# Penalty rows of the two key stacks loaded in unit 13 of SyncE's program, ahead of the stores of the chunk's keys

## The reference, cut to what matters

```python
x = layernorm(x + attn(x))                                # 16 heads, one K and one V for all of them
Q, K, V = x @ Wq.T + bq, ctx @ Wk.T + bk, ctx @ Wv.T + bv  # 1024 queries, 6404 keys, 16 heads of 8
scores = where(mask == 0, -1e9, Q K^T / sqrt(8))
x = layernorm(x + softmax(scores) V @ Wo.T + bo)
x = layernorm(x + top1_expert(x))
```

## Time and profile before

| | |
|---|---|
| median of three runs | 472.44 us (471.43 to 472.73) |
| profiled execution: span | 468.0 us |
| profiled execution: time around its span | not on the page; its only time is the span |
| mean granted TensorE clock | 0.981 |
| PE busy | 441.4 us, 94% |
| DVE (VectorE) busy | 400.8 us, 86% |
| ACT (ScalarE) busy | 359.8 us, 77% |
| POOL (GpSimd) busy | 246.1 us, 53% |
| DMA | 56.07 MB, mean 120 GB/s |

### The profile page before, as it was taken

The page is one execution under the profiler, slowest core; times in us unless marked ns, Lnnn a source line. Parts: engine busy times, 40 slices in busy tenths (PEclk is TensorE's granted clock), DMA queues, the critical chain, the costliest instruction groups (busy, mean ns, idle before and its releaser), DMA issues.

```text
span 468.0 us, 10772 instructions
## 1 busy us (share of the span) xinstructions
PE 441.4 (94%) x3885; PEld 175.9 (38%) x3887; DVE 400.8 (86%) x506; ACT 359.8 (77%) x704; POOL 246.1 (53%) x382
## 2 busy tenths in 40 slices
PE   7999989999999999899999999999999999999973
PEld 2533333333334433233344333333344334343441
DVE  5989989999899698689998999999999899962175
ACT  6328878698867777688868888888868688878843
POOL 4836878976899404222446643454438154321364
PEclk9889999999999999999999999999999899999998
DMA  5859977679760172211322345322222122111001
GB/s 131 322 125 315 278 258 251 265 245 377 260 267 14 36 125 68 67 50 39 89 73 69 114 87 106 90 61 58 81 58 69 39 59 62 50 41 40 5 12 36
DMA packets 24596, 56.07 MB, mean 120 GB/s; under 512 B 6443, under 2 KB 15929, under 8 KB 22493
## 3 DMA queue, kind: packets, MB, share of 16 engines
q0 software_dynamic: 7536, 37.91, 24.9%
q1 hardware_dynamic: 16424, 17.24, 14.2%
q10 hardware_dynamic: 580, 0.20, 0.2%
HBM read 45.60 MB, written 9.18 MB: 117 GB/s over the span
## 4 chain that ended last, share of the span: by engine, by line
PE 69%; DVE 15%; DMA 5%; POOL 4%; issue 4%; ACT 2%; ACTq 0%; DVEq 0%; POOLq 0%
PE O L1491 26%; PE ST L1727 14%; PE RT L1720 7%; PE ST L1518 7%; DVE mxs L938 7%; PE RT L1506 4%; DVE mxc L955 3%; POOL big L612 3%; DMA big<-in_mask 2%; DMA Qs<-mxr 2%; PE RT L1613 2%; PE ST L1620 1%; PE O L1469 1%; DVE mxc L956 1%; PE RT L1583 1%
## 5 line engine op out<-in xcount | busy, mean ns | idle before, releaser
L1290 ACT ACTIVATE prob<-ST 128x512 f32<-128x512 f32 x512 | 280.9, 599 | 59.1 <-PE ST L1518 27.4
L938 DVE TENSOR_REDUCE mxs<-RT 128x2 f32<-128x1024 f32 x128 | 152.8, 1222 | 12.8 <-PE RT L1506 11.7
L955 DVE TENSOR_REDUCE mxc<-RT 128x2 f32<-128x1024 f32 x128 | 152.4, 1219 | 6.6 <-PE RT L1720 6.4
L1727 PE MATMUL ST<-Qs,Kc 64*128 64x512 f32 x320 | 117.8, 451 | 0.0
L1720 PE MATMUL RT<-Kr,Qs 64*128 64x512 f32 (+1 forms) x384 | 114.1, 405 | 2.2 <-issue 2.2
L1491 PE MATMUL O<-prob,vst 128*9 128x256 f32 x1280 | 99.9, 384 | 1.7 <-ACT prob L1279 0.5
L1518 PE MATMUL ST<-Qs,Kself 64*128 64x512 f32 x256 | 96.2, 447 | 2.5 <-DMA Qs<-mxr 2.4
L684 POOL DMA_DIRECT2D Kr<-kd x96 | 47.8, 503 | 85.9 <-PE RT L1720 70.8
L1506 PE MATMUL RT<-Kself,Qs 64*128 64x512 f32 x256 | 88.7, 462 | 2.2 <-DVE Kself L915 0.9
L1491 PE MATMUL O<-prob,Vs 128*9 128x256 f32 x1024 | 80.2, 385 | 1.2 <-ACT osb L1234 0.3
L1727 PEld LDWEIGHTS ST<-Qs,Kc 64*128 64x128 f32 x320 | 50.6, 185 | 66.3 <-issue 36.6
(11 more groups left out here) (219 smaller groups left out, 326.8 us busy)
## 6 DMA issues: line engine op xcount, KB each, us to landing
big<-in_mask POOLq DMA_DIRECT2D x16, 1664.0 KB, 7.6
Kc<-kd POOLq DMA_DIRECT2D x64, 80.0 KB, 2.3
Kr<-kd POOLq DMA_DIRECT2D x64, 64.0 KB, 2.1
od_s<-osb SPq DMA_DIRECT2D x16, 128.0 KB, 2.3
kd<-Vx SPq DMA_DIRECT2D x4, 512.0 KB, 6.7
Qs<-qd_x SPq DMA_DIRECT2D x8, 256.0 KB
od_x<-osb SPq DMA_DIRECT2D x14, 128.0 KB, 1.7
Qs<-qd_s SPq DMA_DIRECT2D x12, 128.0 KB, 5.9
```

What stands on the lines that cost most here:

```text
L938: freed(v.tensor_reduce(mxs[:, h % 2, c2, :].rearrange("p (f t) -> p f t", f=2)[:, :, q], bank[:, :].rearrange("p (f k) -> p f k", f=2), A ...
L955: return v.tensor_reduce(o[:, :, u % 4], src, AX.X, ALU.max)
L1290: freed(nc.scalar.activation(prob[:, s % SLOTS, f * HALF:(f + 1) * HALF], bank[:, :], ACT.Exp))
L1727: mm = mmul(o[:, :], Kc[STACK[f], b * P:(b + 1) * P], Qs[STACK[f], j, :], start=True, stop=not gen, skip_group_check=True)
```

## The change

In SyncE's loop the two waits and the two loads move from the turn `h == 14`, behind `more_keys()`, into the turn `h == 13`, right behind the five stores to `pd`. `more_keys()` stays in `h == 14`.

```diff
                 if h == 13:
                     sp.wait_ge(S("pen_made"), 1)
                     for k, c in enumerate((*range(CHUNKS - 4, CHUNKS), CHUNKS - 5)):
                         load(pd[:, k * KC:(k + 1) * KC], penr[...], "pen_out")
-                if h == 14:
-                    more_keys()
                     sp.wait_ge(S("pen_out"), 16 * 5)
                     sp.wait_ge(S("k_clean"), 2)
                     for k_ in (Kr, Kc):
                         load(k_[PENROWS[0]:PENROWS[1] + 1:PENROWS[1] - PENROWS[0], :].bitcast(F32),
                              pd.to_broadcast([2, KUSE]), "pen_in")
+                if h == 14:
+                    more_keys()
```

## The result

The changed kernel takes 469.13 us (median of 18 executions, 464.88 to 475.08), the kernel before 472.59 (18, 466.89 to 476.76). The ratio is 0.9921, with a 95% interval of 0.9896 to 0.9947. Forecast: 469.1.

What follows compares the result with a forecast made beforehand. TensorE was taken to bound the kernel, 69% of the chain of waits. Stop 2.62 plus low clock 1.49 made 4.11 us, cut to 3.28 by the late split: 472.44 - 3.3 = 469.1 us, range 467.7 to 471.3.

Steps and rivals of the forecast that it cites:

- The wait named by its landing: TensorE's 2.2 us stop at the first cross-row product ends when the last penalty load (`pen_in`) lands, 2.0 us after issue.
- The sum: Stop's excess 2.62 plus slow passage 1.49 make 4.11 us; the late split limits the gain to 3.28 us, giving 469.1 us.
- the end of the split: GpSimd finishes splitting unit 15's maxima at 196.98, after its wait for the chunk's keys; the change does not move this.
- The step of the next late thing: Unit 15's turning would wait for GpSimd's split of its maxima, so the gain is 3.28 us, not 4.11.
- fourth rival: GpSimd's split isn't late because key stores land earlier without penalties behind them: gain up to 4.11, 468.3 us; chance 0.06.
- The low clock: TensorE's half-clock passage in the two steps after the stop, 1.49 us, was taken to go with the stop.
- first rival: The low clock doesn't follow the stop before the first cross row: gain only 1.8, 470.6 us; chance 0.19.
- The cost of 0 on SyncE: Moved wait and loads take 3.4 us within SyncE's 5.68 us idle before unit 14's maxima, so cost nothing.
- the cover: Slack on SyncE's queue: 5.4 us more, beyond its idle time, before TensorE needs unit 14's maxima; key stores stay at 189.39.
- third rival: SyncE is held by the penalties' store round trip, delaying unit 14's maxima: 474.8 us at 5 us beyond the cover; chance 0.03.
- The time around the span: Execution outside the profiled span, taken as 4.44 us (median 472.44 above the span's 468.0) and left unchanged.

Runs made afterwards that it cites:

- early split: Changed kernel with GpSimd's split of unit 15's maxima ahead of its wait for the chunk's keys: 468.19 us, 0.9938; same edit on the kernel before: 473.05 us, 1.0027.
- filled stop: Kernel before, with ten matmuls on constants ahead of the first cross row's wait for the penalties: 472.22 us (0.9996), again 471.36 us (0.9957).
- loads in turn 14: Kernel before, with the two penalty loads kept in turn 14 but put ahead of the key stores: 470.74 us (1.0000), again 470.51 us (0.9978).
- held run: Changed kernel with six more small waited-for stores on SyncE between the penalties' stores and their loads: 470.49 us in one execution.

## Why the prediction was right

**The wait named by its landing: right.** The profile gave no releaser. That `pen_in` ended the stop was argued from an issue time plus a nearby duration (2.0 us); it is 2.0 to 2.1 in six traces of four kernels and for two different loads.

**The sum: right, and its terms nearly so.** Predicted from column to column was 4.68 us (197.50 - 192.82), measured 4.59. What sets it is the end of the split. That was forecast 196.98 - 192.82 = 4.16 us behind the column product and came after 198.34 - 194.13 = 4.21. From there to the next column it took 198.72 - 198.34 = 0.38 us instead of 0.52. In the 0.52, taken from an unwaited turning, the first weight load (183.79) stands 0.21 ahead of the first product (184.00), among products still running; in the waited one both start at 198.39. The three steps ahead of the turning also took longer: their column products stand at 194.13, 195.34 and 196.71, the second step 1.37 instead of 1.22, with a wait for ScalarE that I hadn't looked at (a copy of O at 195.63 goes ahead of the exponential). The wait for the split hid that; it only shortened the turning's wait.

**The step of the next late thing: right, and worth the most.** Without it the sum would have been 4.1 us; the early split gives 0.6 of the difference back, and nothing without the change. My fourth rival falls: the key stores don't land earlier without the penalties behind them (195.69 - 190.70 = 4.99 us to GpSimd's next load, against 194.34 - 189.39 = 4.95 in the earlier trace rows).

**The low clock: right in the trace, uncertain in the whole.** The term was 1.49 us, from one trace. The first rival (the passage doesn't depend on the stop) falls for this stretch by the filled stop. I had also misread the row that spoke for it: between 185 and 188 TensorE was idle for 0.92 us, less than half of the 2.18, not "nearly as much". In none of the seven traces of kernels with the loads ahead and SyncE not held does the distance carry a low passage. But the term isn't a constant: 1.5, 2.7, 3.0. In the whole it looks smaller. Over the 201 executions whose clock is on record, single ones left out, the time within each kernel falls by 4.0 us for each 0.01 of mean granted clock (correlation -0.88). By that slope each kernel can be taken to the same clock and set against before on its own chip, in means of all executions. The changed kernel is then 1.6 and 1.5 us faster than before, the loads in turn 14 1.7 and 1.9, and the filled stop, which keeps the wait, 0.2 and 0.3 slower (standard errors 0.3 to 0.5). That is the pure waiting of the sum, 3.28 - 1.49 = 1.8. The rest is clock: without the correction the changed kernel is 2.8 and 2.4 us faster, so 1.3 and 0.9 us came with its higher mean clock (0.9804 against 0.9773, 0.9802 against 0.9780), below the 1.49 and uncertain by about as much. The medians differ by 3.5, 3.3 and 1.8 us in the three groups. That the first comes so near to the forecast's 3.3 thus owes something to luck in how the low passages fell.

**The cost of 0 on SyncE: right in size, wrong in two parts.** The landing of the stores was mis-sized (0.9 us behind the last issue, not 2.0), on the safe side. And the cover was counted for the wrong instruction. Held 8 us longer, SyncE lost nothing on the maxima, and 2.3 us on the key stores. The third rival's price of 474.8 was reckoned from the maxima, with a threshold of a landing 9.8 us after the last store. The key stores are late earlier, from a landing of about 0.9 + 8.0 - 2.3 = 6.6 us (an estimate from the held run). The real landing takes 0.9 us, and the wait and both issues together hold SyncE for 2.1, so nothing like it happened.

**The time around the span.** I added 4.44 us to the span, taking median and trace as one execution. The profiled execution of the changed kernel has 471.09 us in all around a span of 469.0, so 2.1; the rest was the difference between executions. The forecast didn't suffer, because it was a difference laid on the median.

## What to carry to other kernels

When the profile names no releaser for a stop, look up what the instruction waits for in the code and add the landing time of a like DMA to each issue; an edit that shifts one of them alone settles it. Price a removed wait only up to the next thing that is late, and look for that thing on the queue of another engine, behind the same transfer. Before a step goes ahead on a queue, count the cover of every instruction that it passes, not of the next one alone; and compare traces stretch by stretch, since a passage of low clock far away can hide the whole gain.

## What the runs showed of the hardware

A low passage of TensorE's clock came with a stop of 2.1 to 2.2 us in three of three traces, and cost 1.5 to 3.0 us beyond the stop. A stop of 1.4 us at the same place brought none in its one trace, and ten filler matmuls on constants kept the clock at 1.00 in two of two. At the end of the kernel a stop of 1.5 us was followed by a low passage in nine of thirteen traces, at 3.3 us each, so the length of a stop alone doesn't decide. The Trainium skill ("TensorE: Matmul & The Clock Gate", Part 1) says that the activity monitor runs freely and that one and the same kernel counts a different number of slow matmuls at its start from run to run. The traces agree as far as the length varies, with distances of 16.47, 17.72 and 17.97 us for the same wait; what sets it they don't show.

A store of 1 KB to DRAM, waited for and followed by the next, takes 1.34 us per round trip (one trace, six in a row). A load of 10 KB out of DRAM into two partitions was seen by the waiting engine 2.0 to 2.1 us after the start of its issue, in six traces.
